# Two-pair passes for a second phase of a Strassen matmul: phase 4 joins phase 6

## The reference

```
y   = conv(x, weight, groups=4) + (cond @ c_weight.T)[:, :, None] + fside[None, :, None]
A_eff, B_eff = gate @ lora_A, gate @ lora_B            # one adapter of rank 32 for each batch entry
out = x + y @ kernel + bias + (y @ A_eff.T) @ B_eff.T + (y @ A_shared.T) @ B_shared.T
```

## Time and profile before

| | us |
|---|---|
| median of 3 runs | 1678.27 (1677.45 to 1679.99) |
| the profiled execution, its own time | 1678.24 |
| its span in the trace | 1676.5 |
| PE busy in it | 1662.0 (99%) |
| DVE busy | 1142.5 (68%) |
| ACT busy | 705.7 (42%) |
| POOL busy | 103.3 (6%) |

### The profile page before, as it was taken

One profiled execution on the slowest core, in us unless ns is written; L12 is line 12 of the kernel. 1 busy time (PEld: TensorE's weight loads), 2 busy tenths in 40 slices (PEclk: granted clock), 3 DMA queues, 4 the chain that ended last, 5 costly groups with the idle time before them and its releaser, 6 DMA issues.

```text
span 1676.5 us, 22036 instructions
## 1 busy us (share of the span) xinstructions
PE 1662.0 (99%) x8336; PEld 1419.3 (85%) x8336; DVE 1142.5 (68%) x1627; ACT 705.7 (42%) x916; POOL 103.3 (6%) x142
## 2 busy tenths in 40 slices
PE   9999999999999999999999999999999999999999
PEld 6799988888888899998888888888888888887787
DVE  7888888975445689999996445354555545468776
ACT  7776776645222566656562111132233211223221
POOL 0011110110000000000000242000000000001000
PEclk9999999999999999999999999999999999999999
DMA  8968777976756768877777887577677898998885
GB/s 252 284 224 288 254 239 260 317 272 197 246 202 207 246 193 294 277 242 246 251 243 244 283 315 276 181 232 250 222 228 228 275 330 312 320 314 241 227 227 163
DMA packets 185376, 423.40 MB, mean 253 GB/s; under 512 B 51220, under 2 KB 90740, under 8 KB 180632
## 3 DMA queue, kind: packets, MB, share of 16 engines
q1 hardware_dynamic: 168008, 358.93, 64.1%
q0 software_dynamic: 16256, 58.73, 12.5%
q10 hardware_dynamic: 1008, 4.34, 0.9%
HBM read 271.71 MB, written 150.22 MB: 252 GB/s over the span
## 4 chain that ended last, share of the span: by engine, by line
PE 93%; DVE 4%; DMA 1%; issue 1%; ACT 1%; SPq 0%; DVEq 0%; ACTq 0%
PE acc L1895 61%; PE cps L1764 15%; PE cps L1814 4%; PE cps L1965 3%; PE acc L1965 3%; PE acc L1798 3%; PE acc L1731 2%; PE acc L1848 1%; DVE g L1284 1%; DMA b_raw<-mixed_B 1%; PE acc L1977 0%; DMA g<-A 0%; PE cps L1824 0%; DVE w_lo L1216 0%; DVE x_q L1294 0%
## 5 line engine op out<-in xcount | busy, mean ns | idle before, releaser
L1895 PE MATMUL acc<-w_hi,y_t 128*128 128x512 f32 x3072 | 852.6, 391 | 2.8 <-issue 1.7
L1895 PEld LDWEIGHTS acc<-w_hi,y_t 128*128 128x128 f32 x3072 | 569.3, 188 | 117.2 <-issue 2.9
L1895 PE MATMUL acc<-w_lo,y_t 128*128 128x512 f32 x1536 | 474.2, 390 | 0.0
L1895 PEld LDWEIGHTS acc<-w_lo,y_t 128*128 128x128 f32 x1536 | 288.3, 188 | 61.4
L924 ACT COPY x_q<-x_raw 32x512 f32<-32x512 f32 x248 | 269.7, 1087 | 20.9 <-DVE x_lo L1301 12.2
L1764 PE MATMUL cps<-cw,x_hi 128*128 128x256 f32 (+2 forms) x1088 | 244.0, 313 | 0.4 <-DVE x_lo L1481 0.4
L1764 PE MATMUL cps<-cw,x_lo 128*128 128x384 f32 (+2 forms) x768 | 181.0, 283 | 0.0
L1764 PEld LDWEIGHTS cps<-cw,x_hi 128*128 128x128 f32 x1088 | 176.5, 189 | 3.6 <-DVE x_lo L1481 1.2
L963 ACT CAST y_t<-g 128x1024 fp32r<-128x1024 f32 x79 | 83.3, 1054 | 227.2 <-PE acc L1895 192.7
L1423 DVE TENSOR_TENSOR g<-acc,g 128x1024 f32<-128x1024 f32 x80 | 97.7, 1222 | 110.2 <-PE acc L1798 63.6
L1294 DVE COPY x_q<-x_raw 32x512 f32<-32x512 f32 x248 | 147.9, 596 | 4.4
(11 more groups left out here) (215 smaller groups left out, 1575.9 us busy)
## 6 DMA issues: line engine op xcount, KB each, us to landing
g<-U SPq DMA_DIRECT2D x80, 512.0 KB, 6.3
g<-A SPq DMA_DIRECT2D x72, 512.0 KB, 4.8
A<-g SPq DMA_DIRECT2D x64, 512.0 KB, 4.4
x_raw<-in_x SPq DMA_DIRECT2D x31, 1024.0 KB, 5.1
g<-in_x SPq DMA_DIRECT2D x48, 512.0 KB, 6.2
out<-g SPq DMA_DIRECT2D x48, 512.0 KB, 3.6
...
```

What stands on the lines that cost most here:

```text
L1895: ins = T.matmul(acc[:, b, m, :], y_buf[b][:, c, part, :], wt[:, k % SLOTS, m * 512:(m + 1) * 512], start=(c == 0 and part == 0 and wt is ...
```

## The change

Phase 4 is done as phase 6 is: eight passes over two pairs, r = 0 to 7, and phase 6's passes become r = 8 to 15. The names follow: `first_pair(r)`, `phase_of(r)`, and `step(u)` for the body of the loops over the remaining phases.

- The 14 weight pieces of phase 4 are combinations of T4's quarters. POOL's `combine` forms them in phase 1 (in `x_q`, which it clears at the edges again) and stores them as Z4 to Z7. The piece loads and early splits that stood in phase 5 stand in phase 3 too.
- A pass of phase 4 has eight data parts: a21 is split as well, since Ax needs it. `pass_ax_part` does the 8 Ax matmuls of a pair into half of P7's bank, j = 0 before P4 and j = 1 behind it. Ax, its difference and their splits are made in DVE's and ACT's lists between the parts, with two places for the earlier part and for the difference (`axp_two`, `axd_two`) and one for the split difference (`axd_hl`).
- P4 moves from seventh to third product in all sixteen passes, and the additions, banks and events are renumbered for it.
- The eight weight pieces of phase 5 (T5) are loaded in passes 2 to 7 and split in the last pass of phase 4.

```diff
-LORA_PHASES = (1, 4, 5, 6)
+LORA_PHASES = (1, 5)
+BOTH_LORA = (1, 4, 5, 6)
 AX_PHASES = (0, 1, 3, 4)
+STEPS = tuple(range(1, 4 * NP)) + tuple(range(5 * NP, 6 * NP))
 EARLY_SPLIT = {5: 0, 8: 1, 11: 2}
 PAIR_AT = {2: (0,), 3: (1,), 4: (2,), 5: (3,), 6: (4,), 8: (5,), 10: (6,), 12: (7,), 13: (8,), 14: (9,)}
 PAIR_SPLIT = {5: 0, 7: 1, 9: 2, 11: 3, 12: 4, 13: 5}
-EV_P1, EV_P2, EV_P6, EV_L11, EV_P5, EV_P7, EV_L22, EV_P3, EV_L12, EV_P4, EV_L21 = range(1, 12)
+EV_P1, EV_P2, EV_P4, EV_P6, EV_L11, EV_P5, EV_P7, EV_L21, EV_L22, EV_P3, EV_L12 = range(1, 12)
 EVS = 11
-EV_OF = (EV_P1, EV_P2, EV_P6, EV_P5, EV_P7, EV_P3, EV_P4)
-ADD_E1, ADD_U2, ADD_L11, ADD_P5, ADD_P5B, ADD_U3B, ADD_L22, ADD_U3_21, ADD_L12, ADD_L21 = range(1, 11)
+PARTS = {4: ("a11", "a12", "a22", "a21", "S2", "S1", "S3", "S4"), 6: ("a11", "a12", "a22", "S2", "S1", "S3", "S4")}
+PART_OF = ("a11", "a12", "a22", "S2", "S1", "S3", "S4")
+READ_BY = {"a11": EV_P1, "a12": EV_P2, "a22": EV_P4, "a21": EV_P4, "S2": EV_P6, "S1": EV_P5, "S3": EV_P7, "S4": EV_P3}
+SUM_NO = {"S1": 1, "S2": 2, "S4": 3, "S3": 4}
+ADD_E1, ADD_U2, ADD_L11, ADD_P5, ADD_P5B, ADD_U3_21, ADD_L21, ADD_U3B, ADD_L22, ADD_L12 = range(1, 11)
 ADDS = (("E1", 0, 0, None), ("U2", 0, 1, None), (EV_L11, 0, 0, ADD_E1), (EV_P5, 0, 1, ADD_U2), (EV_P5, 1, 1, None),
-        ("U3", 1, 1, ADD_P5B), (EV_L22, 1, 1, ADD_U3B), ("U3", 1, 0, None), (EV_L12, 0, 1, ADD_P5),
-        (EV_L21, 1, 0, ADD_U3_21))
+        ("U3", 1, 0, None), (EV_L21, 1, 0, ADD_U3_21), ("U3", 1, 1, ADD_P5B), (EV_L22, 1, 1, ADD_U3B),
+        (EV_L12, 0, 1, ADD_P5))
 NADD = len(ADDS)
-LAST_ADD = (ADD_L11, ADD_L22, ADD_L12, ADD_L21)
+LAST_ADD = ((ADD_L11, 0, 0), (ADD_L21, 1, 0), (ADD_L22, 1, 1), (ADD_L12, 0, 1))
...
+            for r in range(QS):
+                more = r + 1 < QS
+                if r >= 1:
+                    for n in range(1, 4):
+                        store_pass(r - 1, n)
+                if more:
+                    for j in range(2):
+                        load_pass_y(r + 1, j)
+                    load_b(first_pair(r + 1))
+                else:
+                    for j in range(2):
+                        load_y(5 * NP + j)
+                if 2 <= r < 6:
+                    load_t(5, r - 2)
+                if r == 1:
+                    load_bias(1)
+                if more:
+                    for j in range(2):
+                        load_pass_out(r + 1, j)
+                else:
+                    load_t(5, 4)
+                    load_t(5, 5)
+                store_two_ax(r, 0)
+                if more:
+                    load_two_ax(r + 1, 0)
+                else:
+                    load_t(5, 6)
+                store_two_ax(r, 1)
+                if more:
+                    load_a(first_pair(r + 1))
+                    load_two_ax(r + 1, 1)
+                store_pass(r, 0)
...
+            def combine(i, c, src, dst):
+                n = NCH + 4 * i + c
+                pool.wait_ge(form_out, 64 * n)
+                V.dma_start(xq_flat[:, 0:HALF], src[c]).then_inc(form_in, 16)
+                V.dma_start(xq_flat[:, HALF:2 * HALF], src[c + 4]).then_inc(form_in, 16)
+                pool.wait_ge(form_in, 64 * NCH + 32 * (4 * i + c + 1))
+                V.tensor_tensor(b22, b22, b12, ALU.subtract).then_inc(form_done, 1)
+                V.tensor_tensor(b12, b12, b11, ALU.subtract).then_inc(form_done, 1)
+                pool.wait_ge(form_done, 4 * n + 2)
+                V.tensor_tensor(b11, b22, b11, ALU.add).then_inc(form_done, 1)
+                pool.wait_ge(form_done, 4 * n + 3)
+                V.tensor_tensor(b21, b21, b11, ALU.subtract).then_inc(form_done, 1)
+                pool.wait_ge(form_done, 4 * n + 4)
+                for buf, to in zip((b22, b12, b11, b21), dst):
+                    V.dma_start(to[c], buf).then_inc(form_out, 16)
+            pool.wait_ge(x_lo_ready, 2 * (NP - 1))
+            for c in range(NCH // 2):
+                combine(0, c, T4_d, (Z7_d, Z5_d, Z6_d, Z4_d))
+            pool.wait_ge(form_out, 64 * (NCH + 4))
+            V.memset(x_q[:, :, :, 0:1], 0.0).then_inc(edge_zero, 1)
+            V.memset(x_q[:, :, :, XW - 1:XW], 0.0).then_inc(edge_zero, 1)
...
+            for r in range(QS):
+                u, first, last = first_pair(r), r == 0, r + 1 == QS
+                b_split(u)
+                if first:
+                    hi_part(r, 3)
+                hi_part(r, 4)
+                pass_copy(r)
+                if first:
+                    split_pair(4, 10)
+                if last:
+                    for c in range(3):
+                        split_t(5, c)
+                copy_ax(ax_index(u))
+                hi_part(r, 5)
+                ax_hi(u)
+                axd_hi(u)
+                if first:
+                    split_pair(4, 11)
+                hi_part(r, 6)
+                if first:
+                    split_pair(4, 12)
+                copy_ax(ax_index(u + 1))
+                hi_part(r, 7)
+                if first:
+                    split_pair(4, 13)
+                if not last:
+                    hi_part(r + 1, 0)
+                ax_hi(u + 1)
+                axd_hi(u + 1)
+                if not last:
+                    a_split(u + 2)
+                    for e in range(1, 4):
+                        hi_part(r + 1, e)
...
+            for r in range(QS):
+                u, first, last = first_pair(r), r == 0, r + 1 == QS
+                if not first:
+                    pass_add(r - 1, ADD_L12)
+                b_split(u)
+                if first:
+                    lo_part(r, 3)
+                lo_part(r, 4)
+                pass_s4(r)
+                if first:
+                    split_pair(4, 10)
+                else:
+                    pass_add(r, ADD_E1)
+                if last:
+                    for c in range(3):
+                        split_t(5, c)
+                sum_ax(u)
+                lo_part(r, 5)
+                pass_s3(r)
+                ax_lo(u)
+                axd_lo(u)
+                if first:
+                    split_pair(4, 11)
+                lo_part(r, 6)
+                if first:
+                    split_pair(4, 12)
+                sum_ax(u + 1)
+                lo_part(r, 7)
+                if first:
+                    split_pair(4, 13)
+                if not last:
+                    lo_part(r + 1, 0)
+                ax_lo(u + 1)
+                axd_lo(u + 1)
+                if not last:
+                    a_split(u + 2)
+                    pass_s1_s2(r + 1)
+                pass_u2(r)
+                if first:
+                    pass_add(r, ADD_E1)
+                pass_add(r, ADD_U2)
+                pass_add(r, ADD_L11)
+                if last:
+                    split_t(5, 3)
+                else:
+                    lo_part(r + 1, 1)
+                pass_add(r, ADD_P5)
+                pass_add(r, ADD_P5B)
+                if last:
+                    split_t(5, 4)
+                else:
+                    lo_part(r + 1, 2)
+                pass_u3(r)
+                if last:
+                    split_t(5, 5)
+                    y_lo(5 * NP)
+                pass_add(r, ADD_U3_21)
+                pass_add(r, ADD_L21)
+                if not last:
+                    lo_part(r + 1, 3)
+                pass_add(r, ADD_U3B)
+                pass_add(r, ADD_L22)
...
+            def one_pass(r):
+                F, first = phase_of(r), r % QS == 0
+                if r == 0:
+                    pe.wait_ge(y_evac, 4 * NV)
+                else:
+                    pe.wait_ge(pass_copied, r)
+                pass_product(r, 0, EV_P1)
+                bank_out(r, ADD_L11)
+                pass_product(r, 1, EV_L11, joined=True)
+                bank_out(r, ADD_L21)
+                sum_out(r, 2)
+                if first:
+                    pe.wait_ge(evac_dve, evac_no(F * NP - 2) + 1)
+                    if F == 6:
+                        pe.wait_ge(evac_u, NP - 1)
+                if F == 4:
+                    pass_ax_part(r, 0)
+                pass_product(r, 2, EV_L21, joined=True)
+                if F == 4:
+                    pass_ax_part(r, 1)
+                sum_out(r, 1)
+                pass_product(r, 3, EV_P6)
+                pass_lora(r, 0, 0, EV_L11)
+                bank_out(r, ADD_P5B)
+                pass_product(r, 4, EV_P5)
+                if F == 4:
+                    pe.wait_ge(ax_both, 3 * NP + 2 * r + 2)
+                pass_product(r, 5, EV_P7)
+                pass_lora(r, 1, 0, EV_L21)
+                bank_out(r, ADD_L22)
+                if first:
+                    pe.wait_ge(evac_dve, evac_no(F * NP - 1) + 1)
+                    if F == 6:
+                        pe.wait_ge(evac_u, NP)
+                pass_lora(r, 1, 1, EV_L22, alone=True)
+                bank_out(r, ADD_L12)
+                pass_product(r, 6, EV_L12, joined=True)
+                pass_lora(r, 0, 1, EV_L12)```

```

(45 more changed lines are left out.)

931 lines of the change are left out of this document (520 added, 411 removed).

## The result

The changed kernel takes **1738.18 us** (median of 6 runs, 1736.54 to 1740.27) against 1678.45 of the kernel before (6 runs, 1675.81 to 1680.12): a ratio of 1.0357, 95% interval 1.0344 to 1.0370. It is slower, as forecast, but by 60 us where 22 were forecast, and outside the range. Its profiled execution took 1739.94, with a span of 1737.7 against 1676.5: 61.2 more, which is what has to be explained.

The account below looks back on a forecast made before the run. Phase 4 passes were taken as bound by DVE's list plus two waits, 27.7 us each. 1678.24 + 22.5 (phase 4) + 2.1 (phase 5's entry) − 2.5 (P4 third) = 1700.3 us, range 1673 to 1724.

Parts of the forecast that it names:

- the ring: Phase 4 passes: DVE, ACT and SP wait for each other; DVE's list plus two uncovered waits sets a 27.7 us period.
- M: Phase 4 passes: time from SP's issue of the first difference's store to its landing, taken as 4.5 us.
- The `axd_hl` wait: Phase 4 passes: ACT may write the second difference only when the first's store has landed; DVE waits 1.5 us.
- x: Length of the `axd_hl` wait in a phase 4 pass: M − 3.0, not under zero; 1.5 us, 0.5 to 3.4.
- The `a_raw` wait: Phase 4 passes: DVE stands still until the next `a_raw`, loaded behind the second difference's store, is there: 1.0 + L.
- L: Phase 4 passes: landing time of the next pass's `a_raw` load, taken as 4.1 us from a row of 2.6 to 6.0.
- Rival 3: Phase 4: both landings slow, `pass_out` loads going out 1.5 us ahead of the first difference's store; 1727 us, chance 0.12.
- Rival 1: Phase 4: queue quiet when the late small transfers go, L 1.8 and x 0; faster, 1674 us, chance 0.17.
- Rival 2: Phase 4: PE and not DVE's waits bounds the passes, which take 22.85 us; 1661 us, chance 0.05.
- Rival 4: The clock falls in new idle gaps of 2.2 us and less; would only add time, its chance counted in Rival 3.
- The combine at zero: Phase 1: POOL's combine costs nothing, as the same work in phase 3 leaves PE full.
- Phase 5's entry: Start of phase 5: B rows, loaded behind the last pass's stores, come late; +2.1 us, 0 to 4.

Follow-up runs that it names:

- experiment 1: The changed kernel with two places for the split difference, so that ACT waits for no store of the same pass: 1715.17 us.
- experiment 2: The changed kernel with the load of `a_raw` issued ahead of the loads of `pass_out`: 1711.51 us.
- experiment 4: The changed kernel with the loads of `pass_out` issued behind both stores and the load of `a_raw`, one place for the difference: 1709.01 us.
- experiment 6: The changed kernel with the stores of the split difference issued by POOL on its own queue instead of by SP: 1710.63 us.
- Experiment 3: The changed kernel with two places for the split difference and the `a_raw` load ahead of the `pass_out` loads: 1689.94 us.
- Experiment 5: The changed kernel with two places for the split difference and the `a_raw` load first of all in each pass of phase 4: 1673.11 us.
- experiment 11: Experiment 5 plus phase 5's first B load in phase 4's last pass and POOL's combine started some 25 us into phase 1: 1660.73 us.
- experiment 8: The kernel before plus POOL's combine of T4's quarters alone, its results stored and read by nobody: 1683.29 us.
- experiments 7 and 10: 7: changed kernel, POOL's combine held until phase 1 has begun, 1736.59 us. 10: Experiment 5 plus that hold and phase 5's first B load earlier, 1664.99 us.

## Why the prediction was wrong in size and right in kind

**Right: the ring and what it is made of.** If the passes are bound by DVE's list and the two waits, the seven intervals less DVE's two waits must be the same in every kernel whose order of loads differs. Sum of the intervals, less both waits, per pass:

| kernel | intervals | `axd_hl` | `a_parts` | rest per pass |
|---|---|---|---|---|
| changed | 223.9 | 41.9 | 28.8 | 21.9 |
| experiment 1 | 201.1 | 0 | 49.5 | 21.7 |
| experiment 2 | 196.5 | 44.1 | 0 | 21.8 |
| experiment 4 | 196.1 | 16.3 | 26.3 | 21.9 |
| experiment 6 | 192.9 | 20.8 | 19.8 | 21.8 |

The list is 21.8, forecast as 21.1 (and 24.0 in the first pass, so 21.5 in the mean). Experiment 3 has 22.2, since three of its seven passes are bound by PE. Experiment 5 shows that other bound at 23.0 (forecast 22.85). These two terms held.

**Wrong: M, the landing of the store, in "The `axd_hl` wait".** I took 4.5 from the stores of the kernel before; in passes 1 to 6 they measured 8.0 to 10.6. The formula x = M − 3.0 held: with 9.3, the mean of the six, it gives 6.3, and 6.2 was measured in these passes. In pass 0, where I had x hidden by the weight splits, it was 4.8. Over the seven intervals x came to 41.9 where six times 1.5 were put in, +32.9. The `a_raw` wait came to 28.8 against 35.7, −6.9 (L was 3.1, not 4.1). DVE's list came to +2.6. The sum, +28.6, is near what phase 4 was above the forecast (+28.1); the last pass was 1.6 shorter than forecast, and phase 4 before the change 203.9 and not 204.8. The fault was to price a store by its own kind in a place where SP had nothing in front of it. Rival 3 saw the 1 MB that goes out 1.5 ahead, and still took 6.4, the slowest of those undisturbed stores, as its bound. The row to read was that of those very loads in phase 6 of the kernel before, where they stand in the same kind of pass:

```profile
L477 SPq DMA_DIRECT2D g<-U x15: 320/387/683, 1499.9 to 1640.6; - x15
...
DMA to landing us min/median/max: 4.1/8.6/9.7
```

What is issued 1.6 behind a load of 8.6 and can't pass it lands in at least 7.0 (in the changed kernel all six stores landed behind both loads). That makes x 4.0 and the time some 17 us more, about 1718, still inside the range; the bound above should have come from 9.7 and from the other loads of the pass.

**Rival 1 and the rule behind it** (a quiet queue, 1674) needed L + x under 2.4; measured was 9.1. The figure of the Trainium skill behind it (DMA: Bandwidth & Descriptors, Anatomy of one DMA), which gave 2.3 for L, stands there for DMAs that GpSimd issues, and this load is SP's: L was 3.1. **Rival 2** (PE bounds, 1661) is what experiment 11 is, at 1660.73: its condition, that the order of the lists allows early loads, was false for the change as it was made. That its price met the time is in part luck: phase 4 takes 190.5 there, where the price has 203.9 − 22.0 + 5.2 = 187.1, and phase 5 is 0.8 shorter than before, where it has 2.1 more. **Rival 3** had the right cause and too small a price. **Rival 4**, the clock: with idle gaps of up to 6.3 it fell, to 0.91 in the window shown of phase 4, where I had counted on gaps of 2.2 at most. What that cost isn't settled, for the ring was DVE's and the rest per pass above is the same at granted clocks from 0.983 to 0.993 over the run.

**The combine at zero: wrong.** I argued from phase 3, where the same work on POOL leaves PE full. There it has cover. At the boundary of phases 0 and 1 it has none, and costs 4 to 6 (experiment 8); 25 us further on it costs nothing (experiment 11). I named a late data load as the risk; it was DVE's own speed, and where the combine was held until phase 1 began, late B rows after all (experiments 7 and 10). The Trainium skill (GPSIMD Engine Reference, Specifications) says that GpSimd shares its SBUF interfaces with VectorE, with contention for VectorE instructions with two SBUF inputs; the splits of W have two, and the trace agrees.

**Phase 5's entry: right in cause, short in size.** B rows came late by the mechanism named, 5.6 instead of 2.1, and the other 2 lie in or behind the window at a granted clock of 0.83. **P4 in third place** was forecast as −2.5 and phase 6 came to −1.7 (−1.6 to −3.8 in the profiles of all the kernels that have this order): the waits of the earlier trace rows are gone. This part was not tried by itself.

**What PE's waits were to show**: idle before the second Ax part (0.9 to 1.7 in seven passes and 4.1 in the last, against a forecast 2.2), before P2 (5.3 each against 1.5), none for `b_two` in the passes. The idle time forecast before the first Ax part, 1.2, wasn't there. An interval of 32.0 less 22.85, 1.3 and 5.3 leaves 2.5 in which PE was busy. The lower clock accounts for about as much (an estimate: 22.85 / 0.91 − 22.85 = 2.3), so PE filled with slower work what had been forecast as idle.

Left open: in experiment 11, phases 5 and 6 together take 364.1 against 368.2 before the change. Of these 4.1, 3.3 are phase 6 (175.1 against 178.4), twice what it gained in the changed kernel, and the cause of that difference is open.
